# A graph, attention and expert layer on one core: adjacency counting with fewer register loads, reordered exponentials and loops placed at fixed slots

## The chip, the cores and the metric

One core of one Trainium2 chip. The metric is the device time of one execution in microseconds; before the change the median of 3 runs is 965.2 us (964.98 to 967.04). Lower is better.

## The reference

The input is 625 nodes of 512 features, and 20625 directed edges (10000 drawn edges both ways and 625 loops) sorted by destination. One step adds a graph network and an attention-like mixer to the residual, the next a layer of 64 experts with 6 per node:

```python
xn = layernorm(x)
x = x + gnn(xn, edges) + mix(xn)
x = x + experts(layernorm(x))

# gnn: three of these layers
m = relu(x[src]) + eps
e = exp(m * t - max)
agg = segment_sum(e * m, dst) / segment_sum(e, dst)
h = agg + x
h = relu(layernorm(h @ w1 + b1)) @ w2 + b2
```

## The kernel before

The nodes stand as 5 tiles of 125 rows. The kernel is written engine by engine, with semaphores by name; nothing is scheduled by a planner. So the order of the work on each engine is the order of its code.

**The mixer's end.** For each tile t of the mixer's attention, TensorE makes the attention sums (`attend`), VectorE divides them (L1273 to L1279), TensorE transposes the quotient (L1729), ScalarE copies it out of PSUM with rounding (L812, semaphore `xt_hi`), VectorE makes the rounded copy's remainder (L1287, `xt_lo`), and TensorE multiplies by the output weights (`mix_out`, through `mm3`, L261 to L263: three matmuls per product, for high and low parts). VectorE adds each result to the output rows (`mix_add`, L1267). `mix_out(4)`, the last, waits for `xt_lo` of tile 4 and for `mix_add(2)`, which frees its PSUM bank.

**The adjacency stage.** Since a segment sum is a product with a matrix, the kernel first counts the edges into a 625 x 625 matrix, once for all three layers. The sorted edges are cut into 165 chunks of 125. Each of the 5 destination tiles goes over its chunks in groups of G = 5; the first chunk and the number of groups of each tile are data. VectorE computes them (`tile_ranges`, L1234 to L1247) into `lohi_i` and they are loaded into registers of TensorE, VectorE and ScalarE, one value at a time:

```python
groups = q.value_load(lohi_i[0:1, 1, j:j + 1], min_val=1, max_val=NG - 1)
before = q.value_load(lohi_i[0:1, 2, j:j + 1], min_val=0, max_val=(NT - 1) * NG) if j else 0
```

(L404, L405, and L410 for the first chunk.) For each chunk VectorE writes a one-hot of the sources (L1316, `source_one_hots`, 125 x 626), ScalarE a step function of the destinations (L860, `destination_steps`, 125 x 126), and TensorE multiplies the two in 5 matmuls (L1797, `count`) into two PSUM banks. There are 5 buffers of each operand; TensorE gives one back per chunk (`one_hot_free`). A tile is one group written out, and a loop over the others (L1331 on VectorE, L870 on ScalarE, L1810 on TensorE). With these inputs each tile has 7 groups, so there are 35 groups and 175 chunks.

On TensorE each tile begins with two matmuls by zeros that open the sums (L1808) and ends with two that close them (L1813, `adj_ps`). Between tiles ScalarE copies the sums out (`adj_copy`, L834 and L836), VectorE takes the difference of neighbouring columns (`adj_difference`, L1304), ScalarE rounds it (L840) and VectorE makes the remainder (`adj_low`, L1309). The PSUM banks alternate.

**Between the two.** ScalarE loads its 14 values after its last copy for the mixer, and then makes the first layer's exponentials of tiles 0 and 1 (`exponential`, L819; then `exponential_hi`, L828, and `weighted_hi`, L824). VectorE loads 5 values behind `mix_add(1)` and 9 behind `mix_add(2)`; then come the remainder of tile 4 (L1287), the products with the exponentials (`exp_times_message`, L1254; `exponential_lo`, L1262), `mix_add(3)`, `weighted_lo` (L1258), and the first one-hots. The exponentials share their memory with the mixer's quotients.

After the stage come the three layers, and then the experts, whose weights stream from memory.

## Time and profile before

| | |
|---|---|
| median of 3 runs | 965.2 us (964.98 to 967.04) |
| the profiled execution's own time | 959.11 us |
| its span, first to last instruction | 957.3 us |
| mixer's end and what follows to the first one-hot | 100 to 119.65 us of the span |
| adjacency stage, first one-hot to first aggregate matmul | 119.65 to 182.60 us |
| mean granted TensorE clock over the span | 0.976 |

Times in rows of the trace are counted from the span's start. In a timeline the columns are start, length in microseconds, engine, line, operation, what it writes and reads, how many merged instructions, and in brackets how long the engine was idle before and what ended that. "issue" means that the engine waited for nothing that the profile shows: its own sequencer was busy with register work. An engine's name with a q is its sequencer.

### The profile page before, as it was taken

The numbers are of one execution on the slowest core, as the hardware profiler recorded it, in microseconds if no ns is written. First come the engines' busy times: TensorE is split into PE (matmuls) and PEld (weight loads), VectorE is DVE, ScalarE is ACT, GpSimd is POOL, SyncE is SP. The second block draws the span as 40 slices with busy tenths as digits, with TensorE's granted clock in tenths as the row PEclk, the third lists the DMA queues.
The fourth block names the chain that finished last, engine by engine and source line by source line (L and its number), as shares of the span: only waits on it lengthen the run. The fifth ranks groups of instructions, "written<-read, shape, count | busy, mean of one in ns | idle before, by whom it ended". The sixth has DMA issues, their size and how long they took to land. (4 is left out here: it accounts for less than half of the span.)

```text
span 957.3 us, 14571 instructions
## 1 busy us (share of the span) xinstructions
PE 888.3 (93%) x4781; PEld 685.5 (72%) x4781; DVE 682.7 (71%) x1145; ACT 498.0 (52%) x866; POOL 380.7 (40%) x326
## 2 busy tenths in 40 slices
PE   4999799999999999989999897999999999999980
PEld 3898588878877788768887786666666666666650
DVE  6966589966546768766778886587677677667675
ACT  2665289935445262452625235556656655655630
POOL 2002000086002650125511264576676676666540
PEclk9999999999999999999999999899999999999995
DMA  6433000242001420013201615699999999999868
GB/s 182 142 122 121 33 1 1 92 152 99 1 1 56 132 88 1 1 59 128 72 1 34 224 67 206 208 335 326 330 343 357 340 328 358 357 358 337 289 179 213
DMA packets 57164, 159.77 MB, mean 167 GB/s; under 512 B 13901, under 2 KB 21651, under 8 KB 48656
## 3 DMA queue, kind: packets, MB, share of 16 engines
q1 hardware_dynamic: 44725, 147.50, 44.6%
q0 software_dynamic: 12288, 11.36, 4.2%
q8 instruction: 34, 0.56, 0.2%
q14 instruction: 26, 0.21, 0.1%
q10 hardware_dynamic: 91, 0.13, 0.1%
HBM read 152.71 MB, written 25.58 MB: 186 GB/s over the span
## 5 line engine op out<-in xcount | busy, mean ns | idle before, releaser
L261 PE MATMUL ps<-split_operands 128*125 128x512 f32 (+5 forms) x690 | 266.7, 387 | 12.6 <-DVE split_operands L1346 4.4
L263 PE MATMUL ps<-split_operands 128*125 128x512 f32 (+5 forms) x690 | 260.8, 378 | 0.0
L262 PE MATMUL ps<-split_operands 128*125 128x512 f32 (+5 forms) x690 | 260.6, 378 | 0.0
L671 POOL DMA_INDIRECT yrow_scratch<-work,row_i x64 | 151.3, 2365 | 96.8 <-ACT work L1009 94.2
L261 PEld LDWEIGHTS ps<-split_operands 128*125 128x125 f32 (+3 forms) x690 | 129.7, 188 | 42.3 <-DVE split_operands L1346 5.1
L263 PEld LDWEIGHTS ps<-split_operands 128*125 128x125 f32 (+3 forms) x690 | 129.7, 188 | 26.5
L262 PEld LDWEIGHTS ps<-split_operands 128*125 128x125 f32 (+3 forms) x690 | 130.1, 189 | 23.6
L1571 DVE TENSOR_TENSOR gate_up_lo<-expert_weights,split_operands 128x2048 fp32r<-128x2048 f32 x64 | 146.1, 2282 | 0.5 <-ACT split_operands L991 0.5
L393 POOL TENSOR_TENSOR split_operands<-work,split_operands 128x512 fp32r<-128x512 f32 x66 | 84.0, 1302 | 144.0 <-ACT split_operands L375 135.1
L991 ACT ACTIVATE split_operands<-expert_weights 128x2048 fp32r<-128x2048 f32 x64 | 121.8, 1903 | 0.0
L2063 PE MATMUL ps<-expert_weights,work 128*117 128x512 f32 x256 | 120.3, 592 | 0.5 <-issue 0.5
L261 PE MATMUL ps<-split_operands,expert_x 128*117 128x512 f32 x256 | 106.6, 417 | 0.1
L263 PE MATMUL ps<-split_operands,expert_x 128*117 128x512 f32 x256 | 101.8, 398 | 0.0
L262 PE MATMUL ps<-gate_up_lo,expert_x 128*117 128x512 f32 x256 | 101.7, 397 | 0.0
L1001 ACT ACTIVATE work<-ps 117x256 f32<-117x256 f32 x64 | 24.5, 384 | 129.0 <-PE ps L263 129.0
L665 POOL DMA_INDIRECT work<-xn_scratch,tok_i x64 | 71.2, 1112 | 22.0 <-issue 22.0
L912 ACT ACTIVATE work<-ps,colp 128x125 f32<-128x125 f32 x120 | 44.0, 467 | 64.3 <-PE ps L1855 64.3
L1369 DVE RECIPROCAL work<-work 125x512 f32<-125x512 f32 x15 | 50.3, 3351 | 34.6 <-ACT work L894 34.6
L2063 PEld LDWEIGHTS ps<-expert_weights,work 128*117 128x117 f32 x256 | 45.9, 180 | 39.3 <-issue 32.5
L1584 DVE COPY work<-ps 128x234 f32<-128x234 f32 x64 | 25.7, 402 | 64.2 <-PE ps L2072 64.2
L1797 PE MATMUL ps<-work 125*125 125x126 bf16 x875 | 56.4, 226 | 4.0 <-DVE work L1316 3.5
L1797 PEld LDWEIGHTS ps<-work 125*125 125x125 bf16 x875 | 54.5, 141 | 6.2 <-DVE work L1316 5.4
(217 smaller groups left out, 1270.4 us busy)
## 6 DMA issues: line engine op xcount, KB each, us to landing
expert_weights<-experts_in SPq DMA_DIRECT2D x64, 1024.0 KB
expert_weights<-experts_in SPq DMA_DIRECT2D x64, 512.0 KB, 8.7
work<-w_in SPq DMA_DIRECT2D x12, 1024.0 KB, 5.1
yrow_scratch<-work SPq DMA_DIRECT2D x5, 1500.0 KB
split_operands<-yrow_scratch SPq DMA_DIRECT2D x4, 1120.0 KB
work<-cw_in SPq DMA_DIRECT2D x3, 1024.0 KB, 5.1
work<-rows_in SPq DMA_DIRECT2D x10, 256.0 KB, 5.2
work<-wmix_in SPq DMA_DIRECT2D x4, 512.0 KB, 5.3
```

The lines of the kernel that those rows point to most:

```text
L261: pe.matmul(o, a[1], b[0], start=start, stop=False)
L262: pe.matmul(o, a[0], b[1], start=False, stop=False)
L263: return pe.matmul(o, a[0], b[0], start=False, stop=stop)
L393: last = pool.tensor_tensor(v[0], v[1], v[2], ALU.subtract)
L665: pool.indirect_dma_start(XG[e % AHEAD], None, xn2, bass.IndirectOffsetOnAxis(ap=tok_i[:, e:e + 1], axis=0), bounds_check=last_token, oob_ ...
L671: pool.indirect_dma_start(yrow, bass.IndirectOffsetOnAxis(ap=row_i[:, e:e + 1], axis=0), OS[e % 4], None, bounds_check=last_row, oob_is_er ...
L912: last = act.activation(RR[:, cut(k * T, T)], ps[:, 2 + h, cut((k % 4) * T, T)], ACT.Relu, bias=colp[:, cut(COL_LB + 8 * L + k, 1)], scale ...
L991: act.activation(GU_hi[e % 2], RING[e % RINGS][:, 0:WA], ACT.Copy).then_inc(S("weight_hi"), 1)
L1369: v1(dve.reciprocal(DEN[d % 2], DEN[d % 2]))
L1571: dve.tensor_tensor(GU_lo[e % RINGS][:], RING[e % RINGS][:, 0:WA], f(GU_hi[e % 2]), ALU.subtract).then_inc(S("weight_lo"), 1)
L1797: last = pe.matmul(ps[0:T, 2 * (j % 2) + s // 4, cut(s % 4 * (T + 1), T + 1)], one_hot_src[:, i, cut(s * T, T)], step_dst[:, i, :], start= ...
L2063: last = pe.matmul(ps[0:CAP, 6 + e % 2, :], HTF[e % 2][:, cut(k * CAP, CAP)], RING[e % RINGS][:, cut(WA + 512 * k, 512)], start=(k == 0), ...
```

## The change

- `tile_values` and `first_chunks` load five values with one instruction (2 loads on ScalarE and on VectorE, 1 on TensorE). The number of groups before a tile is summed in registers and no longer loaded. The first chunks are loaded without a runtime check of their bounds.
- VectorE's loads stand together behind the quotient of tile 4 and its predecessor's remainder; `mix_add(2)` moves from ahead of the remainder of tile 4 to behind it.
- ScalarE makes the exponentials of tiles 0 and 1 ahead of the mixer's copy of tile 3, into another place in memory, and their rounded copies ahead of its own loads; the mixer's copy of tile 4 comes behind the loads.
- The zero matmuls are gone: the first product of each bank opens it, the last closes it, and `adj_copy` waits for the last chunk's `one_hot_free`. TensorE's loop runs one time fewer and the last group is written out behind it. So each tile needs at least 2 groups.
- TensorE's loops begin at slot 0 of a block of 256 instructions. Entering one costs a taken branch over the padding. The loops of ScalarE and VectorE are not placed.

```diff
@@ tile values
-        def tile_values(q, j):
-            groups = q.value_load(lohi_i[0:1, 1, j:j + 1], min_val=1, max_val=NG - 1)
-            before = q.value_load(lohi_i[0:1, 2, j:j + 1], min_val=0, max_val=(NT - 1) * NG) if j else 0
+        def exp_at(L, s):
+            return EE_first[s] if not L and s < 2 else EE[s % 2]
+
+        def tile_values(engine):
+            bound = dict(engines=[engine])
+            _, groups = nc.values_load_multi_w_load_instructions(lohi_i[0:1, 1, :], min_val=MIN_GROUPS, max_val=NG - 1, **bound)
+            before = [0]
+            for n in groups[:-1]:
+                before.append(before[-1] + n + 1)
             return groups, before
...
@@ ScalarE
+            for t in range(3):
+                attn_hi(t)
             act.wait_ge(S("zmax_neg"), 1)
-            act.wait_ge(S("ranges"), 1)
-            tiles = [tile_values(act, j) + (first_chunk(act, j),) for j in range(NT)]
+            for s in range(2):
+                exponential(0, s)
+            attn_hi(3)
             act.wait_ge(S("attn_ps"), NT)
             for s in range(2):
-                exponential(0, s)
-            for s in range(2):
                 exponential_hi(0, s)
+            act.wait_ge(S("ranges"), 1)
+            counts, befores = tile_values(mybir.EngineType.Activation)
+            firsts = first_chunks(mybir.EngineType.Activation)
+            attn_hi(4)
             for s in range(2):
                 weighted_hi(0, s)
...
             def adj_copy(j):
-                act.wait_ge(S("adj_ps"), j + 1)
+                act.wait_ge(S("one_hot_free"), (befores[j] + counts[j] + 1) * G + G)
@@ VectorE
-                if 2 <= t < NT:
+                if 2 <= t < NT - 1:
                     mix_add(t - 2)
...
-                if 2 < t < NT:
-                    for j in (range(2) if t == 3 else range(2, NT)):
-                        tiles.append(tile_values(dve, j) + (first_chunk(dve, j),))
+                if t == NT - 1:
+                    counts, befores = tile_values(mybir.EngineType.DVE)
+                    firsts = first_chunks(mybir.EngineType.DVE)
...
+            mix_add(NT - 3)
             for s in range(2):
                 exp_times_message(0, s)
                 exponential_lo(0, s)
@@ TensorE
-            parts = [(0, 4 * (T + 1)), (1, T + 1)]
-
-            def count(group):
+            counts, befores = tile_values(mybir.EngineType.PE)
+
+            def count(group, first=False, last_of_tile=False):
...
-                                         step_dst[:, i, :], start=False, stop=False)
+                                         step_dst[:, i, :], start=first and not i and s % 4 == 0, stop=last_of_tile and i == G - 1 and s >= 3)
...
-                for h, sn in parts:
-                    last = pe.matmul(ps[0:T, 2 * (j % 2) + h, 0:sn], zero_b[:, 0:T], zero_b[:, 0:sn], start=True, stop=False)
-                count(before)
-                with pe.Fori(1, groups + 1) as q:
+                count(before, first=True)
+                with nc.Fori(1, groups, engines=[mybir.EngineType.PE], head_slot={mybir.EngineType.PE: 0}) as q:
                     count(before + q)
-                for h, sn in parts:
-                    last = pe.matmul(ps[0:T, 2 * (j % 2) + h, 0:sn], zero_b[:, 0:T], zero_b[:, 0:sn], start=False, stop=True)
-                last.then_inc(S("adj_ps"), 1)
+                count(before + groups, last_of_tile=True)
```

**ScalarE between the mixer and the first steps.** Before, the exponentials stand behind the last of fourteen loads (each TENSOR_LOAD with two register instructions, ISA); line 404, 405 and 410 are the loads, 819 the exponential, 828 and 824 the rounded copies.

```order
L404 TENSOR_LOAD lohi_i
L404 ISA x2
L405 TENSOR_LOAD lohi_i
L405 ISA x2
L410 TENSOR_LOAD lohi_i
L410 ISA x2
L819 ACTIVATE work<-work,zmx,colp 125x512 [waits attn_ps]
L819 ACTIVATE work<-work,zmx,colp 125x512
L828 ACTIVATE split_operands<-work 125x512 [waits exp] x2
L824 ACTIVATE split_operands<-work 125x512 [waits em] x2
```

In the change (line 824 is now the mixer's copy, 831 the exponential, 840 and 836 the rounded copies, 411 and 419 the loads):

```order
L824 ACTIVATE split_operands<-ps 128x4x125 [waits xt_tr] x3
L831 ACTIVATE work<-work,zmx,colp 125x512 [waits zmax_neg]
L831 ACTIVATE work<-work,zmx,colp 125x512
L824 ACTIVATE split_operands<-ps 128x4x125 [waits xt_tr]
L840 ACTIVATE split_operands<-work 125x512 [waits exp,attn_ps]
L840 ACTIVATE split_operands<-work 125x512 [waits exp]
L411 TENSOR_LOAD lohi_i [waits ranges]
L411 ISA x10
L419 TENSOR_LOAD lohi_i
L824 ACTIVATE split_operands<-ps 128x4x125 [waits xt_tr]
L836 ACTIVATE split_operands<-work 125x512 [waits em] x2
```

The exponentials moved ahead of the mixer's fourth copy, and two loads stand ahead of its fifth.

**VectorE at the mixer's last tile, in the change** (line 1296 is the quotient of tile 4, 1304 a remainder, 1284 `mix_add`, 1271 and 1279 the products with the exponentials):

```order
L1296 TENSOR_TENSOR work<-ps,rden 125x512 [waits xt_tr,vector_step]
L1304 TENSOR_TENSOR split_operands<-ps,split_operands 128x4x125 [waits vector_step,xt_hi]
L411 TENSOR_LOAD lohi_i
L411 ISA x10
L419 TENSOR_LOAD lohi_i
L1304 TENSOR_TENSOR split_operands<-ps,split_operands 128x4x125 [waits xt_hi]
L1284 TENSOR_TENSOR x_out<-x_out,ps 125x512 [waits x_rows,mix_out_ps]
L1271 TENSOR_TENSOR work<-work 125x512 [waits exp]
```

Before, `mix_add(2)` and nine loads with their checks stood between the two remainders, and five loads ahead of tile 4's quotient.

**TensorE between two tiles.** Before, from the branch that closes a loop to the next tile's opening:

```order
L1810 COMPARE_AND_BRANCH
L1813 MATMUL ps<-work 125x504
L1813 MATMUL ps<-work 125x126
L404 TENSOR_LOAD lohi_i
L404 ISA x2
L405 TENSOR_LOAD lohi_i
L405 ISA x2
L1808 MATMUL ps<-work 125x504 [waits mix_out_add]
L1808 MATMUL ps<-work 125x126
```

In the change the last group's products follow the branch (line 1814), and so do the next tile's, with one register instruction between:

```order
L1814 MATMUL ps<-work 125x126 [waits step,one_hot]
L1814 MATMUL ps<-work 125x126 x4
L1811 ISA [waits mix_out_add]
L1814 MATMUL ps<-work 125x126 [waits step,one_hot]
L1814 MATMUL ps<-work 125x126 x4
L1811 REGISTER_ALU
```

Loads and zero matmuls are gone from between the tiles.

## Rows read from the trace of the kernel before

**Rows 1.** The page's first part: busy time and instructions of each engine.

```profile
PE 888.3 (93%) x4781; PEld 685.5 (72%) x4781; DVE 682.7 (71%) x1145; ACT 498.0 (52%) x866; POOL 380.7 (40%) x326
```

**Rows 2.** The waits from 100 to 185 us: total, times, longest.

```profile
ACT work L819 <- issue: 7.1, 1, 7.1
DVE split_operands L1287 <- issue: 4.4, 1, 4.4
```

**Rows 3.** The timeline from 100 us to the first products of the adjacency stage.

```profile
101.35 0.68 DVE L1267 TENSOR_TENSOR x_out<-x_out,ps 125x512 f32<-125x512 f32 x1
101.47 0.59 ACT L812 ACTIVATE split_operands<-ps 128x500 fp32r<-128x500 f32 x1 [4.04 <-PE ps L1729]
...
101.49 0.50 PE L261 MATMUL ps<-split_operands 128*125 128x512 f32 x1
...
104.15 0.40 PE L263 MATMUL ps<-split_operands 128*125 128x512 f32 x1
104.30 0.17 DVE L1273 TENSOR_SCALAR rden<-ps 125x8 f32<-125x8 f32 x1 [2.27 <-issue]
...
105.59 0.68 DVE L1287 TENSOR_TENSOR split_operands<-ps,split_operands 128x500 fp32r<-128x500 f32 x1 [0.16 <-DVE work L1279]
...
111.25 0.68 DVE L1287 TENSOR_TENSOR split_operands<-ps,split_operands 128x500 fp32r<-128x500 f32 x1 [4.39 <-issue]
...
111.99 0.49 PE L261 MATMUL ps<-split_operands 128*125 128x512 f32 x1 [2.63 <-DVE split_operands L1287]
...
113.97 1.52 ACT L819 ACTIVATE work<-work,zmx,colp 125x512 f32<-125x512 f32 x2 [7.14 <-issue]
...
116.64 0.68 DVE L1254 TENSOR_TENSOR work<-work 125x512 f32<-125x512 f32 x1
117.25 0.69 DVE L1262 TENSOR_TENSOR split_operands<-work,split_operands 125x512 fp32r<-125x512 f32 x1
...
119.65 1.55 DVE L1316 TENSOR_SCALAR work<-work 125x626 bf16<-125x626 f16 x5
...
120.09 2.15 PE L1797 MATMUL ps<-work 125*125 125x126 bf16 x18 [3.20 <-DVE work L1316]
```

**Rows 4.** The loads of line 404: durations in ns (min/median/max), first and last start.

```profile
L404 DVEq TENSOR_LOAD <-lohi_i x5: 299/304/549, 100.9 to 109.4; - x5
L404 DVEq FUSED_REGOPS  x5: 183/183/229, 101.5 to 109.7; - x5
```

**Rows 5.** Windows: length, busy us of PE, PEld, DVE, ACT, POOL (instructions), PE clock.

```profile
120.10:123.60 3.50, 3.50 (x33) 3.50 (x34) 3.27 (x10) 2.00 (x5) 0.00 (x0) 0.51 0.02 5
123.60:127.00 3.40, 3.40 (x60) 3.40 (x59) 3.15 (x11) 3.02 (x10) 0.00 (x0) 1.00 0.00 0
```

**Rows 6.** The timeline of the adjacency stage, tiles 0 to 4.

```profile
132.34 0.43 PE L1813 MATMUL ps<-work 125*125 125x504 bf16 x2
...
134.61 0.97 DVE L1316 TENSOR_SCALAR work<-work 125x626 bf16<-125x626 f16 x3 [1.42 <-PE ps L1797]
...
142.11 1.56 DVE L1316 TENSOR_SCALAR work<-work 125x626 bf16<-125x626 f16 x5 [0.20 <-PE ps L1797]
...
143.87 1.56 DVE L1316 TENSOR_SCALAR work<-work 125x626 bf16<-125x626 f16 x5 [0.20 <-PE ps L1797]
...
148.16 1.56 DVE L1316 TENSOR_SCALAR work<-work 125x626 bf16<-125x626 f16 x5 [0.54 <-PE ps L1797]
...
158.23 0.81 DVE L1309 TENSOR_TENSOR split_operands<-work,split_operands 125x625 fp32r<-125x625 f32 x1
...
158.95 10.66 DVE L1316 TENSOR_SCALAR work<-work 125x626 bf16<-125x626 f16 x35
...
181.67 0.81 DVE L1304 TENSOR_TENSOR work<-work 125x625 f32<-125x625 f32 x1
```

**Rows 7.** TensorE's loop branch, all tiles: duration in ns (min/median/max).

```profile
L1810 PEldq COMPARE_BRANCH  x30: 76/208/253, 123.8 to 181.9; - x30
```

**Rows 8.** DMA issues over the span: KB each, median us from issue to landing.

```profile
work<-rows_in SPq DMA_DIRECT2D x10, 256.0 KB, 5.2
```

More of the change, by code:

```diff
@@ L36 @@
 NG = CH // G
+MIN_GROUPS = 2
 E = 64
@@ L171, in gps_kernel @@
         EE = [fg(11264 + 512 * i, D, p=T) for i in range(2)]
+        EE_first = [fg(9728 + 1024 * i, D, p=T) for i in range(2)]
         EP = [fg(12288 + 512 * i, D, p=T) for i in range(2)]
@@ L809, in _, with attn_hi @@
             pq_square(7)
-            for t in range(NT):
+            def attn_hi(t):
                 act.wait_ge(S("xt_tr"), NT + t + 1)
@@ L863, in _ @@
             for j in range(NT):
-                groups, before, lo = tiles[j]
+                groups, before, lo = counts[j], befores[j], firsts[j]
                 destination_steps(before, lo, j)
@@ L1326, in _ @@
             for j in range(NT):
-                groups, before, lo = tiles[j]
+                groups, before, lo = counts[j], befores[j], firsts[j]
                 source_one_hots(before, lo)
@@ L1797, in count @@
                         last = pe.matmul(ps[0:T, 2 * (j % 2) + s // 4, cut(s % 4 * (T + 1), T + 1)], one_hot_src[:, i, cut(s * T, T)],
-                                         step_dst[:, i, :], start=False, stop=False)
+                                         step_dst[:, i, :], start=first and not i and s % 4 == 0, stop=last_of_tile and i == G - 1 and s >= 3)
                     last.then_inc(S("one_hot_free"), 1)
             for j in range(NT):
-                groups, before = tile_values(pe, j)
+                groups, before = counts[j], befores[j]
                 if j >= 2:
```

18 lines of the change are left out of this document (10 added, 8 removed).

## The prediction

> **What bounds the kernel now.** The page's first part says that TensorE is busy for 93% of the span [rows 1]. That would make its idle time the only prize. But this share is a mean over stages, and the change touches one stretch, from about 101 to 183 us, so I read that stretch alone: first who waits there, then the timeline, then the windows at the low clock.
>
> The waits name the cause directly. The two longest end in "issue": ScalarE is held for 7.1 us ahead of its exponentials and VectorE for 4.4 us ahead of a remainder [rows 2]. Those are the loads of register values. The timeline shows what hangs on them [rows 3]. VectorE starts tile 4's quotient only at 104.30, 2.27 us late, and tile 4's remainder at 111.25, 4.39 us late; TensorE sits idle for 2.63 us until 111.99, and ScalarE's exponentials start at 113.97. VectorE's first one-hot comes at 119.65 and the first product at 120.09. So up to there the **path is VectorE's queue**, fed by loads and then by ScalarE's exponentials.
>
> In the stage itself, TensorE looks full in the timeline, but VectorE sets the pace. In tile 3 it writes 35 one-hots in 10.66 us without a wait [rows 6], 1.52 us per group of 5. From 119.65 to 181.67 it takes 62.0 us for five such tiles, whose pure work is 5 x 10.66 = 53.3, plus five operations of the kind at 158.23 (three differences and two remainders, each 0.72 from its start to the next start) = 3.6, plus `mix_add(4)`, 0.6: 57.5 us. **4.5 us of the 62.0 are lost to others.**
>
> **Term 1, the start of the stage.** I time the changed queue from the row at 101.35, before which nothing changes except that ScalarE makes its exponentials earlier, in a gap of 4.04 us ahead of 101.47 [rows 3]; two of them need 1.52.
>
> - VectorE ends `mix_add(1)` at 102.03. The quotient's three steps took from 104.30 to 105.43 (0.16 before 105.59), so now they end at 103.2 and the remainder of tile 3 runs from 103.3 to 104.0.
> - Then the loads. Before, one value took a TENSOR_LOAD of 0.30, a register instruction of 0.18 [rows 4] and a short check; 14 values in 7.14 us are 0.51 each. Now the loads are 2 and the pairs behind them 5. Upper bound: 2 x 0.40 + 5 x 0.30 = 2.3 us, where 0.40 and 0.30 share the 0.51 and count a start twice. Lower: 2 x 0.30 + 5 x 0.05 = 0.9, if the pair's length was mostly waiting for its load. I take 2.0, nearer the upper, because the instructions of a pair are the same as before. They begin behind the dispatch of the remainder, so VectorE is free at 105.6.
> - TensorE ends `mix_out(2)` (last matmul at 104.15), transposes tile 4 at once, as its quotient is ready at 103.2, and ScalarE, whose loads also end at about 105, copies it by 105.6.
> - VectorE: remainder of tile 4 at 105.7, then `mix_add(2)`, four operations with the exponentials, `mix_add(3)` and two `weighted_lo`: eight steps behind it at 0.61 (116.64 to 117.25), so the first one-hot at 111.2 and the remainder at 105.7 are nine starts apart: 105.7 + 9 x 0.61 = **111.2 against 119.65, 8.5 us earlier**. `mix_add(2)` is now between the remainder and `mix_out(4)`, which waits for it. It ends at 107.0, while TensorE is busy with `mix_out(3)`, twelve matmuls that take 2.7 us from first start to last (101.49 to 104.15) and so end at about 107.9 from a start at 104.9: hidden, with 0.9 us of cover. TensorE's own load of five values follows `mix_out(4)`, which ends at 110.9, and takes up to 1.6 (0.1 of it ahead of that end, as its sequencer runs ahead); it could be ready at 112.4, 0.8 after the first one-hot is written at 111.6, which five buffers absorb.
>
> The Trainium skill (Runtime: NRT & Kernel Launch, Instruction fetch mechanics) says that a register load costs about 200 ns per register even in bulk. Its estimate for two loads of five is then 2.0 us for the loads alone, some 1.4 more than two rows of 0.30 make, and the result 1.4 us later. No row here has a load of several values.
>
> **Term 2, lost time in the stage.** (a) Between tiles TensorE closes (132.34), loads and opens again; VectorE fills its 5 buffers and waits 1.42 at 134.61 and 0.54 + about 0.15 at 148.16. At later boundaries its 1.44 us of differences and remainders hide this. With no loads and no zero matmuls there, 2.1 us go. What remains between tiles is a taken branch into the loop. The nearest row is the loop's own branch, 208 ns [rows 7]; five are 1.0 us of TensorE's time, hidden, since its 25 products take less than VectorE's 1.52 us. (b) From 120.10 to 123.60 TensorE has the 1.2 GHz clock (0.51), after being idle 3.20 us before the first product; 33 matmuls in 3.5 us, against 60 in the 3.4 behind at 2.4 GHz [rows 5, 3]. Now its idle time there is 1.4 us or less. What is left of the 4.5 us for this, 4.5 - 2.1 - 1.2 from (c), is 1.2. I count 1.0 of it as won. (c) In tile 1 the groups are 1.76 us apart (142.11 to 143.87) where tile 3 has 1.52: five times 0.24 = 1.2. VectorE idles "for TensorE" there, but it is one loop of five with the same code and load; I read it as the place of VectorE's loop in the instruction memory. The change does not place that loop, only moves it up. It can vanish, stay, or come to two tiles: -1.2 to +1.2. I take 0.
>
> **Term 3, the end.** The closing matmuls (0.43) no longer stand ahead of the last `adj_copy` and the aggregates: 0.4 us. The copy in turn starts the chain of exponentials that the next products wait for, so it passes on.
>
> Everything after the stage waits by semaphore for what is before it, so the gain is not lost later; the expert weights start when buffers are released, and shift as well.
>
> **Sum.** 8.5 + 2.1 + 1.0 + 0.4 = 12.0 us. The profiled execution took 959.1 (span 957.3), so it would take 947.1; the median of the runs shown is 6.1 higher, and I subtract from that: 965.2 - 12.0 = **953.2 us**.
>
> **Rivals.**
> 1. *Loads cost per value.* Each of the five values pays its full 0.51 on VectorE: 2.6 for the first load and 1.5 for the second, so 2.1 more than my 2.0; TensorE's own loads are late as well. For it: the sequencer handled values strictly one behind another [rows 4]. Against: one instruction, one round trip. Time: 953.2 + 2.1 to 3, 955.3 to 956.2.
> 2. *VectorE stays throttled by its partners or its placement.* The clock falls again (1.0), and a second loop is slow (1.2), and ScalarE, whose copies between tiles now come on top of steps, takes VectorE's place as the bound with 0.3 per tile (1.5): up to 956.9.
> 3. *More than counted.* The slow loop vanishes (1.2) and the loads take 0.9 (1.1): 950.9.
> 4. *The jumps miss (slower than before).* Each of TensorE's five loops starts in another block of instructions. If the target is not there when TensorE branches, it waits for a transfer. I have no row of such a miss; the nearest is the landing of a small DMA, 5.2 us [rows 8], and below it nothing. VectorE's five buffers cover 1.5 of each. At 5.2 the loss is 5 x (5.2 - 1.5) = 18.5, less the 12.0: 971.7 us. It decides from 12.0 / 5 + 1.5 = 3.9 us per miss. Against: each loop head is in the block behind the one TensorE is in, and 12 us pass per tile. The same page and section of the Trainium skill say that a branch to a target outside the current two-block window stalls for a fetch; the next block is within that window, so the rule does not give this case by itself.
>
> **How the numbers follow.** Forecast 952 to 954.8: 0.52. Rival 1: 0.13. Rival 2: 0.15. Rival 3: 0.15. Rival 4: 0.05, of which 0.03 slower than before. The range takes the first four with their edges and the 1.7 us that one stretch of low clock more or less costs elsewhere: 949.8 to 957.5. A measurement of this kernel tells about 0.2%, 1.9 us, from no change. Faster by more than that 0.95, within it 0.02, slower 0.03.
>
> **What would show it.** The first one-hot near 111.2; the waits on issue at most 2.3 us each; no idle TensorE at the fourth tile's `mix_out`; 35 one-hots per tile in about 10.7 us with no wait for TensorE at the tile boundaries; the first aggregate at about 171 instead of 182.6; and no low clock in the first products. I am wrong on term 1 if the first one-hot is behind 113, on term 2 if VectorE needs over 60 us for the stage, and on the whole if TensorE shows a wait on "issue" of over 1 us at each loop's start.

## The result, and the profile after

The change takes **959.17 us** (median of 6 runs, 956.81 to 960.98), the kernel before beside it 965.56 (964.98 to 967.04, 6 runs): a ratio of 0.9928 [0.991, 0.9946] (of the means, as all ratios here), and by the medians **6.4 us faster**. The forecast was 12.0 us faster, and the result lies 1.7 us outside its range.

The profiled executions mislead when their ends are compared: the span is 959.2 us after and 957.3 before. So I follow the difference of single marks. The first aggregate product comes at 176.06 us, where it came at 182.60: 6.5 us are gained by then, and 6.2 are still there at 540 us. Then the profile after loses 7.7 us in one stretch of low clock (from 6.2 ahead to 1.5 behind), which the profiled execution of the kernel before did not have. Most of its timed runs seem to have it, by their time and mean clock. That stretch is a story of its own, told with the last experiments.

The page's first part shows the same work, less the 20 zero matmuls [rows 1]:

```profile
PE 890.2 (93%) x4761; PEld 688.8 (72%) x4761; DVE 683.0 (71%) x1145; ACT 498.5 (52%) x866; POOL 381.1 (40%) x326
```

The waits of 100 to 185 us, total, times, longest. ScalarE's 7.1 us and VectorE's 4.4 us on issue [rows 2] have become one of 2.9 on VectorE. But TensorE has a wait on issue that it did not have, and ScalarE and VectorE have long waits for TensorE:

```profile
ACT work L877 <- PE ps L1814: 5.4, 6, 3.2
...
DVE work L1332 <- PE ps L1814: 4.4, 10, 2.3
...
PE ps L1814 <- issue: 3.2, 1, 3.2
DVE split_operands L1304 <- issue: 2.9, 1, 2.9
```

The timeline from the mixer's end to the first loop (start, length, engine, line, operation; in brackets the idle time before). It answers to [rows 3]. The view ends at 118 us, so its last rows count only what had begun by then:

```profile
102.83 0.68 DVE L1304 TENSOR_TENSOR split_operands<-ps,split_operands 128x500 fp32r<-128x500 f32 x1 [0.16 <-DVE work L1296]
...
106.42 0.68 DVE L1304 TENSOR_TENSOR split_operands<-ps,split_operands 128x500 fp32r<-128x500 f32 x1 [2.91 <-issue]
...
107.84 0.47 PE L263 MATMUL ps<-split_operands 128*125 128x512 f32 x1 [0.51 <-DVE x_out L1284]
...
111.82 1.55 DVE L1332 TENSOR_SCALAR work<-work 125x626 bf16<-125x626 f16 x5
...
112.25 1.67 PE L1814 MATMUL ps<-work 125*125 125x126 bf16 x25 [1.40 <-DVE work L1332]
...
117.08 1.20 PE L1814 MATMUL ps<-work 125*125 125x126 bf16 x15 [3.16 <-issue]
117.70 0.40 ACT L877 ACTIVATE work<-work 125x126 bf16<-125x126 f16 x1 [3.24 <-PE ps L1814]
117.72 0.39 DVE L1332 TENSOR_SCALAR work<-work 125x626 bf16<-125x626 f16 x1 [2.29 <-PE ps L1814]
```

Up to 112.25 this is the forecast's picture, 0.6 us late. Then TensorE makes its first 25 products and stands still for 3.16 us, until 117.08. Between the two lies its jump into the first loop. Line 1825 is that loop; its instructions of all tiles (duration in ns, min/median/max) have one branch of 3.28 us among 30, where the longest was 253 ns [rows 7]:

```profile
L1825 PEldq COMPARE_BRANCH  x30: 76/216/3282, 113.5 to 174.3; - x30
```

Behind the standstill the granted clock was at the 1.2 GHz level for 3.4 us, which answers to [rows 5] (stretch, length, busy us of PE, PEld, DVE, ACT, POOL, PE clock):

```profile
117.90:121.30 3.40, 3.40 (x36) 3.40 (x34) 2.63 (x8) 2.70 (x8) 0.00 (x0) 0.50 0.00 0
121.30:124.70 3.40, 3.40 (x59) 3.31 (x57) 3.15 (x11) 3.27 (x12) 0.00 (x0) 1.00 0.00 0
```

The loads themselves (lines 411 and 419) now read so, where single ones took 0.30 [rows 4]:

```profile
L411 DVEq FUSED_REGOPS  x5: 183/183/222, 104.3 to 105.5; - x5
...
L411 DVEq TENSOR_LOAD <-lohi_i x1: 1440/1440/1440, 102.9 to 102.9; - x1
...
L419 DVEq TENSOR_LOAD <-lohi_i x1: 611/611/611, 105.8 to 105.8; - x1
```

And VectorE in tile 2 shows the slow loop that was in tile 1 [rows 6], with groups 1.76 us apart, while tile 4 keeps nearly its pace:

```profile
142.34 1.56 DVE L1332 TENSOR_SCALAR work<-work 125x626 bf16<-125x626 f16 x5 [0.28 <-PE ps L1814]
...
144.10 1.55 DVE L1332 TENSOR_SCALAR work<-work 125x626 bf16<-125x626 f16 x5 [0.20 <-PE ps L1814]
145.87 1.56 DVE L1332 TENSOR_SCALAR work<-work 125x626 bf16<-125x626 f16 x5 [0.21 <-PE ps L1814]
...
164.50 11.02 DVE L1332 TENSOR_SCALAR work<-work 125x626 bf16<-125x626 f16 x35
```

One table carries the rest of the text. For the profiled execution of each kernel it gives the start of the first one-hot, VectorE's time for the 35 one-hots of each tile (start of the first to end of the last), and the length of the stage (first one-hot to first aggregate product), all in us. The kernels below the change are those of the experiments:

| kernel | first one-hot | tile 0 | tile 1 | tile 2 | tile 3 | tile 4 | stage |
|---|---|---|---|---|---|---|---|
| before | 119.65 | 12.09 | 13.78 | 11.54 | 10.66 | 10.80 | 62.95 |
| the change | 111.82 | 15.09 | 11.58 | 11.88 | 10.86 | 11.02 | 64.24 |
| unplaced | 111.42 | 11.26 | 11.78 | 11.87 | 10.69 | 10.99 | 60.40 |
| slot 32 | 111.08 | 14.78 | 11.62 | 11.88 | 10.94 | 11.08 | 64.11 |
| slot 70 | 112.46 | 11.25 | 11.50 | 11.88 | 10.89 | 11.02 | 60.30 |
| shifted | 112.58 | 11.27 | 11.82 | 11.14 | 10.73 | 10.81 | 59.57 |
| shifted, aligned rows | 111.11 | 11.25 | 11.85 | 11.12 | 10.70 | 10.71 | 59.41 |
| before, TensorE's loads once | 119.18 | 13.02 | 12.75 | 11.00 | 10.67 | 10.80 | 62.31 |

The change's tiles 1 and 2 take 23.5 us together where they took 25.3. What is missing stands in its tile 0, 3 us longer than before.

### The profile page after: what moved, and what is told of

Same layout as the page of the kernel before. It is cut to its first block and busy times, and to the rows that moved or that the text cites. A ratio compares the mean times of both kernels' runs of the same rounds, so it can differ in the third digit from the quotient of the medians.

```text
span 959.2 us, 14451 instructions
## 1 busy us (share of the span) xinstructions
PE 890.2 (93%) x4761; PEld 688.8 (72%) x4761; DVE 683.0 (71%) x1145; ACT 498.5 (52%) x866; POOL 381.1 (40%) x326
```

## Experiments: the jump into the first loop

The theory after the first profile was that the jump to slot 0 misses the instruction memory, once, in tile 0: the instructions at its target are not there yet. The rival was that what tile 0 loses has another cause (the clock, or the register sums ahead of it).

**Unplaced loops.**

```diff
-with nc.Fori(1, groups, engines=[mybir.EngineType.PE], head_slot={mybir.EngineType.PE: 0}) as q:
+with nc.Fori(1, groups, engines=[mybir.EngineType.PE]) as q:
```

> The change without the placing of TensorE's loops; all else as in the change. In the change's trace TensorE's branch into its first loop took 3.28 us and its matmuls idled 3.16 us on issue; the stage from the first one-hot (111.82) to the first aggregate (176.06) took 64.2 us against 62.9 before. Theory A (the jump goes to a block of instructions that is not there yet): no branch over 0.3 us, the stage takes about 61 us, and the median falls by about 3 against the change. Theory B (TensorE would have had to fetch that block anyhow, when it runs over the boundary): the 3.3 us appear inside the first loop and the stage stays at 64.

Measured: 953.67 us (948.41 to 955.09, 6 runs), ratio 0.9861 [0.9824, 0.9898], where the change itself, run again on that chip below, had 954.67. So the medians are 1.0 us apart and not the 3 that I expected, and their runs overlap too widely to tell. The stage tells more: 60.40 us in place of 64.24. TensorE goes from its first 25 products into the loop with 0.39 us of idle time, and tile 0 takes 11.26 us in place of 15.09. TensorE's timeline:

```profile
111.86 1.67 PE L1814 MATMUL ps<-work 125*125 125x126 bf16 x25 [1.36 <-DVE work L1332]
...
113.91 6.28 PE L1814 MATMUL ps<-work 125*125 125x126 bf16 x96 [0.39 <-DVE work L1332]
```

**Slot 32 in place of slot 0.** The head is later in the same block.

> The change with TensorE's loops at slot 32 of a block in place of 0. By the built program's count the first loop's head would stand 9 slots ahead of a multiple of 256. Theory A1 (slot 0 made the jump go one block further than the next, slot 32 lies in the next, which is there): no long branch, stage about 61 us, as without placing. Theory A2 (every first jump over a boundary misses): a branch of about 3.3 us again, stage 64.

Measured: the longest branch 2.91 us, TensorE idle 2.78 us behind the first 25 products, tile 0 14.78 us; 951.76 us (950.65 to 959.54, 6 runs). So the slot's number within that block is not what matters. The median looked better than that of the unplaced kernel, and its runs lay 9 us apart: four from 950.7 to 951.9 and two at 958.1 and 959.5. No wait in the stage explained that; it is taken up with the two groups of runs.

**Slot 70.** Here the padding ends in the block that TensorE is already in.

> The change with TensorE's loops at slot 70. Slots 0 and 32 both missed (branch of 3.28 and 2.91 us). Theory A3: the branch into the first loop itself stands at about slot 50 of its block, so slots 0 and 32 are both in the next block, which is not fetched yet, while slot 70 is in the same block: no long branch, stage from first one-hot to first aggregate about 60.5 us as unplaced. Rival A2: any placed first loop misses: 3 us again, stage 64.

Measured: longest branch 0.33 us, tile 0 11.25 us, stage 60.30; 956.77 us (947.72 to 959.8, 8 runs). Taken branches into a placed loop cost nothing to speak of, when they don't miss.

**Slot 0 kept, TensorE's code 20 instructions later** (of these waits, two go into one instruction), so that the branch stands later in its block and the jump is the same in form. ScalarE and VectorE load their first chunks ahead of their trip counts here, to see which of the two loads is dear.

```diff
+for _ in range(40):
+    pe.wait_ge(S("pool_consts"), 1)
```

> The change (slot 0) with 20 TensorE instructions more at the program's start, and the two loads of five in the other order on VectorE and ScalarE. Theory A3: TensorE enters the last block 20 instructions earlier, and the fetch of the next has begun or ended when the branch comes: the branch takes clearly less than 3.3 us. Rival A2: 3.3 us again. Loads: if a first load of five is slow as such (1.3 to 1.4 us against 0.6), the first chunks' load now takes 1.3 to 1.4; if it is a matter of the row that is read, it stays at 0.6.

Measured: longest branch 0.32 us, stage 60.26, one run of 956.5 us. The transfers of instructions point to the reason. In the change a packet of 16 KB, which I take for TensorE's next block, starts at 114.51 us, a microsecond *after* the branch began at 113.53, and the products resume at 117.08; here one starts at 108.7, long before the branch. So in the change the transfer of the block had not begun when the branch wanted it. I read the cause as TensorE having only just come into the block ahead of it: in the built program the branch is about the 50th instruction of its block. No row shows when the block was asked for. At later tiles the same kind of jump took 0.29 to 0.30 us. On the load: the first chunks took 0.85 us on VectorE as the first load and the trip counts 1.20 as the second, so the dear row stays dear, and being first adds about 0.25 (0.85 for the first chunks where they took 0.61 as the second load, 1.44 for the trip counts where they took 1.20).

## Experiments: which part of the change gives what

**The start alone** (the change with the stage of TensorE as it was: zero matmuls, the loop over all groups, `adj_ps`; loads once, loops not placed).

> Only the first half of the change: loads of five values, exponentials and loads moved; TensorE's loops and zero matmuls as before, unplaced. Theory (the gain is all in the start): first one-hot at 111.8, stage from first one-hot to first aggregate 61 to 63 us, the median 7 to 9 below before, so below the change. Rival (the stage part gives back little but is needed against stalls at the tile boundaries): VectorE's waits at the first two boundaries (1.4 and 0.7) return, stage 63, median about 958.5.

Measured: 957.12 us (955.35 to 959.8, 9 runs); first one-hot 111.80, stage 60.68. Against the unplaced kernel's 60.40, **leaving out the zero matmuls was worth 0.3 us in the stage**, and it lies at its end: 1.00 us from the last one-hot's end to the first aggregate, where the unplaced kernel has 0.56. The rest of the gain over 62.95 I put down to the missing loads and the missing low clock. I had expected a median below the change's; it is 2.5 us above the change's on that chip (954.67) and 3.5 above the unplaced kernel's, while the two profiles are 0.7 us apart at the first aggregate and 2.0 at their ends (spans of 955.3 and 953.3), most of the rest by a longer stretch of low clock at 403 us (6.8 against 3.4). So the zero matmuls' 0.3 us does not explain the medians.

**The change again, on that chip.**

> The change once more, on this chip. The branch into the first loop takes 3.3 us again if it is a matter of place, and the low clock between 537 and 555 us of its profiled execution is there or not by chance: both theories leave the median 6 to 7 below before.

Measured: 954.67 us (950.49 to 962.4, 6 runs) with before at 966.65, so 12.0 us below it and not 6 to 7 (why, stands with the two groups of runs); longest branch 3.55 us, tile 0 16.54. The miss is there in every profile of a kernel with its first jump to slot 0 from that place, so it belongs to the program.

**Late exponentials** (ScalarE's order of before, in the unplaced kernel: five copies, loads, exponentials).

> Unplaced, with ScalarE's order of before: all five copies of the mixer, then its loads of five, then the exponentials of tiles 0 and 1. Theory (the reordering is worth what ScalarE's loads and exponentials would add to the path): ScalarE's exponentials start at about 108.5, VectorE's products with them about 1.8 us later than at 107.6, first one-hot at 113.2 to 113.8 against 111.4 to 111.8. Rival (VectorE is the path and hides it): first one-hot stays at 111.8.

Measured: 956.45 us (953.69 to 959.75, 7 runs); first one-hot 113.91, 1.5 us behind slot 70's and 2.5 behind the unplaced kernel's. ScalarE's timeline has the wait of rows 2 back, 2.62 us long in place of 7.14:

```profile
105.02 0.59 ACT L824 ACTIVATE split_operands<-ps 128x500 fp32r<-128x500 f32 x1 [2.94 <-PE ps L1744]
108.22 1.52 ACT L831 ACTIVATE work<-work,zmx,colp 125x512 f32<-125x512 f32 x2 [2.62 <-issue]
```

I had expected the first one-hot at 113.2 to 113.8. So of the 8 us at the start, the loads, with VectorE's new order around them, give some 6 (113.91 against 119.65), and the early exponentials 1.5 to 2.5.

**TensorE's loads alone, in the kernel before.**

```diff
+_, counts = nc.values_load_multi_w_load_instructions(lohi_i[0:1, 1, :], engines=[mybir.EngineType.PE], min_val=1, max_val=NG - 1)
...
-    groups, before = tile_values(pe, j)
+    groups, before = counts[j], befores[j]
```

> Edit: the kernel before, with TensorE alone loading its five trip counts once ahead of its tiles, everything else (single loads on VectorE and ScalarE, order of ScalarE, zero matmuls) as before. Theory (term 2: TensorE's single loads between tiles delay the first aggregate product of a tile and with it VectorE): the waits of VectorE at a tile's start (1.42 and 0.69 us before) fall under 0.3, the adjacency stage falls from 62.95 to 60.7 to 61.3 us, the time by 1.5 to 2.3. Rival (the zero matmuls and the buffers of the tile before keep the stall): the stage falls by under 0.5 us and VectorE's waits stay over 0.6.

Measured: 965.62 us (954.95 to 967.6, 10 runs), ratio 0.9984 [0.9959, 1.0009]: no difference that can be told. But the mechanism of term 2(a) holds. VectorE's waits for TensorE from 125 to 185 us fall from 3.3 us, longest 1.4, to

```profile
DVE work L1316 <- PE ps L1801: 1.8, 7, 0.4
```

and tiles 1 and 2 get faster by 1.03 and 0.54 us: 1.6 where I counted 2.1. Tile 0 lost 0.9 of it in this execution, under 6.8 us of low clock where the kernel before had 3.4. My expectation for the stage (60.7 to 61.3) was missed at 62.31, and that for the longest wait (under 0.3) at 0.4; without tile 0's loss the stage would have been 61.4.

## Experiments: the slow loop and the price of a load

In VectorE's slow loop, the next instruction of its sequencer begins 319 ns after the start of the closing branch and in the others 191. In the kernel before the slow loop is that of tile 1, in the change that of tile 2. ScalarE has one too: tile 0 in the kernel before (236 ns where its others have about 155), tile 4 in the change (265). The theory: it is the place of the loop in the instruction memory.

**Shifted.** VectorE's loops 16 instructions later, ScalarE's 13, otherwise the unplaced kernel.

```diff
+for _ in range(26):
+    act.wait_ge(S("zmax_neg"), 1)
...
+for _ in range(32):
+    dve.wait_ge(S("iota"), 3)
```

> Unplaced TensorE loops, and 16 instructions more ahead on VectorE and 13 on ScalarE (waits that are long fulfilled), so that no loop of theirs spans a multiple of 128 slots by my reckoning from which loops were slow. Theory P (the slow back edge is a matter of place): VectorE's next instruction comes 191 ns after each closing branch in all five tiles (319 in tile 2 without the shift), ScalarE's 155 (265 in tile 4), stage 1.2 to 1.5 us shorter than the 60.4 of the unplaced kernel. Rival Q (it is something of the third tile itself): tile 2 stays at 319, stage 60.4.

Measured: 955.56 us (948.94 to 958.83, 6 runs). VectorE's 319 is gone from all tiles, its tile 2 falls from 11.87 to 11.14, the stage from 60.40 to 59.57. Its last three groups of tile 2 come 1.69, 1.52 and 1.50 us behind the ones before them, in place of 1.75 to 1.77. The timeline merges the last four:

```profile
141.07 6.27 DVE L1336 TENSOR_SCALAR work<-work 125x626 bf16<-125x626 f16 x20 [0.21 <-PE ps L1818]
```

ScalarE's tile 4 stayed at 265. Sixteen added instructions that do nothing made the stage faster; so the slow loop is a matter of place, as term 2(c) read it, and of 0.7 to 0.8 us, not 1.2. The median is 1.2 us under that of slot 70 (956.77) on the same chip, but both sets of runs spread over some 10 us, so it shows nothing by itself.

**Aligned rows.** The row of trip counts began at byte 20 of `lohi_i`. Padding each row of five to eight words puts it at byte 32.

```diff
-lohi_i = sb("lohi_i", [1, 3, NT], I32)
+lohi_i = sb("lohi_i", [1, 3, 8], I32)
```

> Edit: the unplaced kernel, with the five integers of each row padded to eight words, so that the second row (trip counts) starts at byte 32 of its partition and no longer at byte 20. Theory (the address makes a load of five values dear): VectorE's first load of five, 1.44 us in the change, falls to 0.75 to 0.9, ScalarE's and TensorE's (1.32, 1.42) with it, the loads of 0.6 stay; VectorE's wait before its first one-hot falls from 2.9 to about 2.2 us, the first one-hot comes 0.4 to 0.7 us before that of the unplaced kernel beside the same start, and the span falls by as much. Rival (the first load after the wait is dear, whatever the address): 1.44 stays 1.4, nothing moves by over 0.1 us.

Measured: VectorE's load of the trip counts

```profile
L411 DVEq TENSOR_LOAD <-lohi_i x1: 843/843/843, 103.4 to 103.4; - x1
```

in place of 1440 ns. That is what the row at byte 0 took as the first load (851 ns), so the place of the row explains the whole difference between the two. The wait ahead of the remainder is 2.31 us in place of 2.92. Both are as expected. The first one-hot came at 111.78, not earlier than the unplaced 111.42, which misses the expectation: this execution reached the loads 0.98 us later, and from the start of the load it is 8.36 us where it was 8.98. The time, of two runs, is 953.18 us (948.51 to 957.85).

**Both, with ScalarE shifted by 16.**

> Edit: the shifted kernel (no fixed slots, VectorE's loops 16 instructions later) with the padded rows, and ScalarE's loops 16 instead of 13 instructions later, so that none of its five loop heads stands where its fifth did. Theory (a loop whose back edge lies across a boundary of the instruction fetch costs 110 to 130 ns more per round): ScalarE's next instruction after its closing branch takes 150 to 160 ns in all five tiles (265 in the fifth of the shifted kernel), VectorE's 191 in all five, the adjacency stage takes 59.0 to 59.6 us, and with the padded rows the time is 0.5 to 1.2 us under that of the shifted kernel: 951 to 955 us. Rival (the stage is bound by VectorE and PSUM copies regardless of ScalarE's back edge): ScalarE's 265 goes and the stage stays 59.6 within 0.2.

Measured: 954.64 us (947.69 to 955.96, 6 runs), before beside it 966.61: 0.9857 [0.9822, 0.9893]. Stage 59.41, tiles 3 and 4 10.70 and 10.71, the pace of [rows 6] with nothing on top. Tile 1 keeps 11.85: there ScalarE's copies of the sums (0.57 and 0.25 us at 123.79) stand among its steps, TensorE waits for ScalarE twice (0.29 us each), and VectorE for TensorE by 0.30, 0.36 and 0.23. The first aggregate comes at 170.52 us, **12.1 us before that of the kernel before**. ScalarE's 265 left tile 4, and tile 0 got 237: I moved the slow loop from one tile to another, where I had expected none.

**The change a third time.**

> The change itself, once more, beside the three kernels above. If the missed jump of TensorE into its first loop is a matter of the program and not of the execution, its branch into the loop takes 2.9 to 3.6 us again and the adjacency stage 64 to 66 us; rival: in this execution it takes 0.3 us and the stage 60 to 61. The time: 955 to 960 us, 2 to 4 us behind the shifted kernel with padded rows on the same chip.

Measured: 954.93 us (950.08 to 962.78, 8 runs), 0.3 us behind the shifted kernel with aligned rows where I had expected 2 to 4; the stage is 62.20. The branch takes 2.63 us, less than expected, but no low clock follows it in this execution, and tile 0 takes 13.16 us:

```profile
112.98 1.67 PE L1814 MATMUL ps<-work 125*125 125x126 bf16 x25 [1.40 <-DVE work L1332]
...
117.15 3.05 PE L1814 MATMUL ps<-work 125*125 125x126 bf16 x47 [2.50 <-DVE work L1332]
```

Against 11.26 the miss costs 1.9 us by itself, and 3.8 to 5.3 with a stretch of low clock behind it (15.09, 16.54). That the low clock comes with the miss shows in the other profiles: of the six with a missed jump four have it there, behind branches of 2.91 to 3.55 us, and the two with the shortest branches (2.33 and 2.63) do not; of the eleven profiles of kernels with the new start and without the miss none has it there. The idle time is put down to VectorE here, which in the same stretch waits up to 1.6 us for TensorE; the branch is what held both.

## Experiments: the two groups of runs

By now the change had 20 timed runs: 7 from 950.1 to 952.8 us, with mean clocks of 0.981 to 0.984, and 13 from 956.8 to 962.8, at 0.969 to 0.978. The main comparison above drew six of the upper group for the change, and 965 to 967 for the kernel before. On the two later chips the change drew both groups, and there the medians lie 12.0 and 11.7 us under the kernel before (954.67 against 966.65, ratio 0.9888 [0.984, 0.9937]; 954.93 against 966.61, ratio 0.9897 [0.9856, 0.9937]), with the same missed jump in the kernel. The other kernels spread as widely. The windows of 536 to 552 us show the difference. First the change's first profile, then its third:

```profile
536.00:544.00 8.00, 5.65 (x28) 5.65 (x29) 4.91 (x12) 1.56 (x4) 2.02 (x5) 0.61 1.01 366
544.00:552.00 8.00, 8.00 (x34) 7.50 (x34) 4.25 (x21) 2.28 (x2) 0.25 (x1) 0.50 0.50 207
```

```profile
536.00:544.00 8.00, 7.54 (x62) 7.21 (x63) 6.51 (x30) 3.71 (x4) 0.87 (x2) 1.00 1.03 376
544.00:552.00 8.00, 8.00 (x41) 6.43 (x40) 6.04 (x15) 2.49 (x7) 7.46 (x6) 1.00 0.28 117
```

The stretch at 1.2 GHz is 17.1 us long in the first and absent in the third. It follows an idle time of TensorE ahead of the last final transposes. Here are those of the first:

```profile
534.92 0.59 PE L1964 MATMUL ps<-ident,x_cur 125*128 125x125 f32 x4
...
538.35 1.09 PE L1964 MATMUL ps<-ident,x_cur 125*128 125x125 f32 x4 [2.84 <-DVE x_cur L1445]
```

The third had 2.38 us there without the fall, and so had the kernel before with 2.86. Of the 15 profiles of kernels with this idle time, 13 have the stretch (10.2 to 17.1 us long), so the fall is frequent and not certain. To test it I filled that wait with nine matmuls of data that is there, into the bank that the transposes overwrite:

```diff
-pe.wait_ge(S("fin_norm"), t + 1)
+if t != 4:
+    pe.wait_ge(S("fin_norm"), t + 1)
...
+if t == 4:
+    for k in range(3):
+        mm3(ps[0:T, FT_BANK[t], :], sub(XF, A_, k, cut(0, T)), sub(SG[0], A_, k, A_), True, True)
+    pe.wait_ge(S("fin_norm"), t + 1)
```

Shifted kernel with aligned rows, filled:

> Edit: the shifted kernel with padded rows, and nine matmuls of data that is there (into the PSUM bank that the next transposes overwrite) in TensorE's wait ahead of the final transposes of tile 4. Theory (the stretch of low clock at 534 us follows the idle time of 2.4 to 2.9 us there and makes the two groups of runs): the idle time falls under 1 us, the stretch is gone from the profile, and all timed runs are in the fast group: 946 to 950 us at a clock of 0.98 or more, median about 948. Rival (the stretch comes from the load of the chip at that time, not from the idle time): the runs keep their two groups, 947 to 949 and 954 to 956, and the profile may show low clock at 534 to 548 with TensorE busy ahead of it.

Measured: **949.24 us (948.36 to 950.54, 6 runs)**, 0.9849 [0.9816, 0.9881]. Mean clock 0.980 to 0.982 in all of them. I had expected about 948. The change, filled:

> Edit: the same nine matmuls, in the change itself. Theory: all runs in the change's fast group, 949.5 to 953 us, median about 951.4. Rival: two groups as before, 950 to 953 and 957 to 963.

Measured: 953.5 us (952.06 to 955.26, 6 runs), where I had expected 949.5 to 953 with a median of 951.4. Its runs are above the lower group of the unfilled change (950.1 to 952.8), and they fall in two sets of their own: three at 952.1 to 952.6 with a mean clock of 0.983, three at 954.4 to 955.3 with 0.978 to 0.979. The profile of the first has a branch of 2.33 us, no low clock behind it and a tile 0 of 12.84 us. The kernel before, filled:

> Edit: the same nine matmuls, in the kernel before. Theory: the kernel before has its two groups from the same place (profiled execution 959.1 without the stretch, most timed runs 965 to 968), so now all runs are 957.5 to 960.5, median about 959; the change's advantage over it is then 959 - 951.4 = 7.6 us. Rival: most runs stay at 964 to 968.

Measured: 960.8 us, the median of 11 runs from 957.5 to 962.4, ratio 0.9971 [0.9945, 0.9997], where 11 of 17 without the filling were at 965 to 967; I had expected 959. A twelfth took 1141.9 us at a mean clock of 0.747 and is left out. The unfilled base, beside them:

> The shifted kernel with padded rows, unedited, beside the three. Both theories: two groups, 947 to 949 us and 954 to 956, with the stretch of low clock at 534 us in the profile of the latter. It serves as the base of the first run.

Measured: 951.56 us (947.73 to 954.23, 6 runs), with 10.2 us of low clock at 535.4 in its profile. Spread 6.5 us, against 2.2 filled. The theory holds: the stretch is in none of the five profiles of filled kernels (two of them follow), against 13 of 15 without the filling, and in these three kernels the upper group of runs is gone. The last transposes come as long behind the ones before them as they did (3.45 us, against 3.43 in the change's first profile), so the filling delays nothing there. That the filled medians came out 1 to 2 us above what I expected from the lower groups is not explained. The first filled kernel, at 2.4 GHz through the transposes (0.64 us, against 1.09 in the change's first profile) and what follows:

```profile
532.47 0.64 PE L1973 MATMUL ps<-ident,x_cur 125*128 125x125 f32 x4
532.95 1.86 PE L1987 MATMUL ps<-router_weights,split_operands 128*125 128x64 f32 x16
```

With most of that noise gone, the missed jump can be priced in the time itself, though few runs are left for it. The filled change with slot 70, and the filled change with slot 0 beside it:

> Edit: the change with the nine filling matmuls and TensorE's loops at slot 70 in place of slot 0. Theory (the missed jump is 1.9 us of tile 0 and up to 3.8 where low clock follows): TensorE's longest branch 0.33 us, tile 0 11.2 to 11.3 us, the stage 60.2 to 60.5, and the median 2 to 4 us under that of the change with the filling beside it: 949.5 to 951.5, all runs within 2.5 us. Rival (what tile 0 loses is regained at later waits): median within 1 us of the other's.

> The change with the nine filling matmuls, once more, as the base of the run before. Both theories: 952 to 955.5 us, TensorE's first jump into a loop 2.6 to 3.6 us.

Measured: 951.06 us (949.45 to 952.89, 4 runs, a wider spread than the 2.5 us expected) against 954.02 (952.17 to 955.59, 5 runs). Tile 0 takes 11.22 against 15.42 us in these two profiles (12.84 in the first profile of the filled change), the longest branch 0.31 against

```profile
L1825 PEldq COMPARE_BRANCH  x30: 76/213/3522, 113.9 to 175.1; - x30
```

**The medians put the missed jump at 3.0 us.** With runs that overlap (949.45 to 952.89 against 952.17 to 955.59) this is a rough price; it lies between the 1.6 to 1.9 us of tile 0 without the low clock and the 3.5 to 5.3 with it. Filled against filled, the change is 7.3 us faster than the kernel before (960.8 to 953.5), and the shifted, aligned version 11.6.

## Why the prediction was wrong

**Term 1, the start: right but for the loads.** Forecast 111.2, measured 111.82, 7.8 us earlier in place of 8.5. The queue behind the loads took its 5.4 us for nine starts, as counted. The step that failed is "I take 2.0": VectorE's loads took 3.5 us (from 102.9, behind the remainder's dispatch, to 106.42). The upper bound of 2.3 fell too, and its error was to price a load of five values at 0.40, the share of a single one. It took 0.61 in one row and 1.44 in the other, and 0.84 when that row was aligned. The pairs behind it kept the length that the rows had shown, 0.28 each. The Trainium skill's price (Runtime: NRT & Kernel Launch, Instruction fetch mechanics) of about 200 ns per register gives, as an estimate, 2.0 us for the two loads of five. They measured 1.44 + 0.61 = 2.05 together, much nearer to it than to my 0.80, though one price per register does not tell the two rows apart. So rival 1's premise was true in part, and its result (2.1 us on top of my 2.0) too large: 1.5 came on top. The first one-hot was only 0.6 us late, because the loads began 0.7 us earlier than counted. The order of the work at `mix_out` nearly held: TensorE was idle 0.51 us there where 2.63 were. It waited for `mix_add(2)`, which I had called hidden with 0.9 us of cover; the late loads had used that up.

**Term 2(a), the waits between tiles: right in the main.** VectorE's 1.42 and 0.54 us are gone; 1.6 of the 2.1 us are shown by the kernel with TensorE's loads alone. The zero matmuls had no part in it that can be seen: the start-alone kernel has them, and its tiles 1 to 4 take 45.2 us together (its own profile), the unplaced kernel's 45.3. In tile 1 a wait of 0.45 us for TensorE remains, and the unplaced, shifted and aligned versions still need about 1.1 us more there than in tile 3. By the waits of the last version a part of rival 2 is in it: ScalarE's copies, which I had not priced in the sum.

**Term 2(b), the low clock: wrong in the change.** I let it go with the idle time ahead of the first products. That went, from 3.20 to 1.40 us, and the clock stayed at 2.4 GHz there: tile 0 without the miss takes 11.26 us, 0.8 less than before, where I counted 1.0. But the missed jump put 3.16 us of idle time a little later, and the low clock came back behind it, as it did in four of the six profiles with a miss.

**Term 2(c), the slow loop: right as a mechanism.** It moved from tile 1 to tile 2 and stayed one, so 0 was the right sum, by luck: I had no row that told where it would land. Its size was 0.8 us by the shifted kernel, not 1.2.

**Term 3: 0.3 us** (0.55 from the last one-hot's end to the first aggregate, where it was 0.84), forecast 0.4.

**Rival 4 is what happened, once.** This is the step that broke the sum: "What remains between tiles is a taken branch into the loop. The nearest row is the loop's own branch, 208 ns." For the first tile that is 3.28 us. I priced the miss at up to 5.2 us by a far row and multiplied by five, which made the rival a slower kernel with little chance. The argument against it, that each loop head is in the block behind the one TensorE is in, and 12 us pass per tile, is true from tile 1 on and false for tile 0: there TensorE had entered its block some 50 instructions before the jump. I had leaned on the Trainium skill there as well (the same page and section): it says that a branch to a target outside the current two-page window stalls for a fetch, and I took the next block for one inside the window. The trace does not bear that reading out for a block that has just been entered: the branch took 3.28 us. I had no mixed case of one miss. Its price without low clock is the branch less what the buffers cover: branches of 2.63 and 2.33 us cost tile 0 1.9 and 1.6, so the buffers covered 0.7 and not the 1.5 that I gave them. With the low clock behind it the change's first profile lost 3.8.

The sum with what was measured, in the change's first profile: 12.0 - 0.7 (loads and start) - 3.8 (missed jump with clock) - 0.5 (rest of 2(a)) - 0.2 (rest of 2(b)) - 0.1 (term 3) = 6.7 us, against 6.5 at the first aggregate and 6.4 in the medians. With the miss and the misplaced loop gone and the row aligned, the same mark is 12.1 us ahead. That this equals the forecast is partly luck: it has the slow loop's 0.8 us and the aligned row, which the forecast did not count, and lacks what is left in tile 1. The forecast's "wrong on the whole if TensorE shows a wait on issue of over 1 us" named the sign; it came at one loop and not at each.

**The end of the range.** I gave 1.7 us to the low clock elsewhere. The stretch at 535 us moves an execution by some 7 to 8 us, and the change falls on either side: its 20 runs have a median of 957.6 us. With the lower group alone it would have seemed to hit the forecast, with the missed jump in it. The kernel before shows both groups too (957.5 to 962.4 and 965.0 to 967.1 among the 17 runs beside the filled kernels), so the ratio of medians depends on how many of each were drawn. A range for this kernel needed that width.

What stays open: why the same idle time is followed by the fall in one execution and not in the next; when TensorE's next block is asked for; and the instruction memory's rule for VectorE and ScalarE, which is only seen from outside, in which loops were slow.

## What to carry to other kernels

A jump over padding was cheap here only where the block behind it had been fetched: look at the first jump after straight code, by the longest of the loop's branch rows and the engine's idle time on issue in its first round. Price a load of several register values by a row of its own and its address, not by that of a single value. Before medians a few microseconds apart are compared, look for a stretch of low clock that some executions have and others not, and for the idle time ahead of it.

## What the runs showed of the hardware that I had not expected

- A missed jump of TensorE took 2.3 to 3.5 us on its branch (2327 to 3547 ns in six profiles of three kernels). One that hit took 0.29 to 0.33.
- On VectorE a load of five values, as the first of two, took 1.44 us from byte 20 of its tensor, 0.84 from byte 32 and 0.85 from byte 0; as the second it took 1.20 from byte 20 and 0.61 from byte 0.
- A loop took 128 ns more on every back edge on VectorE (319 against 191), and 80 to 110 more on ScalarE (236 to 265 against 155), by its place alone: other tiles had it when instructions were added ahead.
- Adding 16 instructions ahead of a stage made it 0.8 us faster. Nine added matmuls made the kernel before 4.5 us faster by its median (965.35 to 960.8) and 2.8 by the ratio of the means. In the shifted kernel the median went from 951.56 to 949.24, which its spread does not resolve, and the spread from 6.5 to 2.2 us.
